# A recurrence whose input terms VectorE and ScalarE write into PSUM, in place of TensorE's injection products

## The chip, the core and the metric

The kernel runs on one core of a Trainium2 chip (trn2). The metric is the device time of one execution in microseconds. Five engines are spoken of: PE (TensorE), DVE (VectorE), ACT (ScalarE), POOL (GpSimd) and SP (SyncE, which only issues DMAs here).

## The reference

```python
def cell(h, x):
    gi = x @ W_ih + b_ih
    gh = h @ W_hh + b_hh
    i_r, i_z, i_n = jnp.split(gi, 3, axis=-1)
    h_r, h_z, h_n = jnp.split(gh, 3, axis=-1)
    r = jax.nn.sigmoid(i_r + h_r)
    z = jax.nn.sigmoid(i_z + h_z)
    n = jnp.tanh(i_n + r * h_n)
    h_new = (1.0 - z) * n + z * h
    return (h_new, h_new)
_, hs = jax.lax.scan(cell, initial_state, xs)
...
logits = flat_x @ Wg + bg
...
h = jax.nn.gelu(tok @ W1[i], approximate=False)
y = h @ W2[i] * p
out = out.at[sel_idx].add(y)
...
x = x + _L0_ffn_ref(_L0_cond_ref(cond_2048, x, ...), ...)
```

The input has 4 sequences of 512 positions and 512 features. A GRU runs over the 512 positions; its states (2048 rows) go to a router that gives each of four experts (512 to 2048 to 512 features) its 512 best rows; the experts' outputs are added to x. All in fp32 accuracy.

## The kernel before

**Segments.** The recurrence is cut into 16 segments per sequence (SEG = 16), so that 4 x 16 = 64 columns (COLS) advance together, 32 positions each (L = 32). As a segment's start isn't known, 8 steps of burn-in and one whole round of 32 go ahead of the round of 32 whose states count: FIRST + L = 72 steps, numbered 0 to 71. A check at the end would start further rounds; they aren't entered with this input.

**What is in a step.** The 512 features of the state are four blocks of 128 (j, or k where they are read). For each block j TensorE makes three gates (r, z, n) of 64 columns in PSUM bank j, `gate_ps`, as sums over the four blocks k of the old state. Numbers are scaled by powers of two and split into a high and a low half of 16 bits. In a rough step (i below ROUGH = 20) only high times high is made: 4 x 4 units of 3 products, 48. In an exact step a unit with the high half of the state takes both halves of the weights (6 products), one with the low half takes the high weights (3): 16 x 6 + 16 x 3 = 144 products of 128x128 by 64 columns, in the order of the table `ORDER`, chosen by hand. The unit (h, j, k) adds to gate bank j what state block k contributes; the last one of each j counts up `gates_mm`.

**Input terms.** x @ W_ih is made for all steps by 512-column products: chunk 3 of four ahead of the recurrence (L424 and L434, in fp32), the others by split halves, `fill` (L451), 24 products ahead of step 0 and then 18 in each step until step 22, which has 12. In a rough step they are dealt out over the k blocks (FILLS = 13, 2, 2, 1), in steps 20 to 22 they stand ahead of the step. ScalarE takes a finished tile of 512 columns out of banks 4 to 7 (`keep_tile`). Tiles of r and z land in a ring `gi_full`, and VectorE splits them in `rz_high` (L1128) and `rz_low` (L1135) into 16-bit halves `gi_rz`. Tiles of n stay fp32 in `gi`.

**Injection.** `inject` (L465 to L473) opens gate bank j of a step: TensorE multiplies `diag`, a diagonal matrix with the scale, by the step's 128 columns of `gi_rz`. It is one product in a rough step, two (high, low) in an exact one, and there a third (L472) adds the recurrent bias b_hn, which was loaded as a row and split by `split_bhn`. In a rough step VectorE adds b_hn instead, in L1248. An injection waits for `rn_done`: VectorE has read the bank's old gates.

**The other engines in a step** (block by block):

- ScalarE: `sig` (L779), one sigmoid of r and z, 128 columns; `tanh` (L784), 64 columns. Order: sig 0, sig 1, sig 2, tanh 0, tanh 1, sig 3, tanh 2, tanh 3. In 16 of the steps 29 to 48 it then squares a 512-wide piece of the first expert weights (L799), with an accumulator.
- VectorE: `reset` (L1245, r times the n gate), `candidate_in` (L1253), `one_less_z` (L1257, (z - 1) n), `blend` (L1264, the new state's high half), and in exact steps `keep_state` (L1269, the new state in fp32) and `low_part` (L1288, its low half for blocks 2 and 3). 16 instructions in a rough step, 22 in an exact one, in the order of the tuples `rough` and `exact`. `blend` and `keep_state` multiply by -s, a pointer scalar (`neg_scale`), and add.
- GpSimd: `carry` (L952, z times the old state) for four blocks, then `low_part` (L960) for blocks 0 and 1.

Each engine works its own list off in order; semaphores are all that ties them. From step 40 on TensorE makes the router's logits of the last state behind the gates (L479).

## Time and profile before

| | |
|---|---|
| median of 3 runs | 836.57 us (836.47 to 837.41) |
| profiled execution | 836.27 us, of which the span is 834.5 us |
| PE, DVE, ACT, POOL busy | 803.0, 619.8, 421.1, 179.9 us |
| granted TensorE clock, mean | 0.987 of full speed |
| first sigmoid of step 0 | at 61.2 us |
| last sigmoid of step 71 | at 439.3 us |

Times in the profile's rows are microseconds from the span's start, and then the duration; "x126" is the number of instructions merged into the row, and "[1.14 <-...]" the idle time of the engine before it and what ended it. PE rows are matmuls, PEld their weight loads. L numbers are lines of the kernel before.

### The profile page before, as it was taken

How to read it: one execution, taken by the hardware profiler on the slowest of the kernel's cores; microseconds unless marked ns; L12 is line 12 of the kernel's file. 1: busy time of each engine (PE TensorE's matmuls, PEld its weight loads, DVE VectorE, ACT ScalarE, POOL GpSimd, SP SyncE). 2: the span in 40 equal slices, each digit the busy share in tenths (PEclk: the TensorE clock that was granted, in tenths of full speed). 3: DMA queues.
4: the chain of work that ended last, by engine and by line, in shares of the span. 5: the costliest groups of instructions: out<-in, count | busy, mean ns of one | idle time of the engine just before them, and what ended most of it. 6: DMA issues, size and time to landing. Idle time of an engine off the chain costs nothing.

```text
span 834.5 us, 28320 instructions
## 1 busy us (share of the span) xinstructions
PE 803.0 (96%) x11781; PEld 528.0 (63%) x11782; DVE 619.8 (74%) x2113; ACT 421.1 (50%) x885; POOL 179.9 (22%) x459
## 2 busy tenths in 40 slices
PE   7999999999999999999995799999999999999996
PEld 3446556679999999999994444454445444444442
DVE  6979899878888888888888879767666676755300
ACT  0677666645566556554455448252835184417400
POOL 1002222123433334333330010121012101210011
PEclk9999999999999999999997899999999999999998
DMA  9810000000111010000001943471347224630022
GB/s 336 323 48 2 2 2 3 2 3 4 54 60 50 17 42 5 4 4 5 5 4 33 269 156 119 135 226 27 113 139 194 57 101 151 171 81 1 1 26 26
DMA packets 24286, 62.64 MB, mean 75 GB/s; under 512 B 4386, under 2 KB 4386, under 8 KB 22308
## 3 DMA queue, kind: packets, MB, share of 16 engines
q1 hardware_dynamic: 19312, 51.42, 18.1%
q0 software_dynamic: 3584, 8.42, 5.5%
q8 instruction: 87, 1.43, 0.7%
q10 hardware_dynamic: 1268, 1.08, 0.4%
q14 instruction: 35, 0.29, 0.1%
HBM read 52.50 MB, written 12.62 MB: 78 GB/s over the span
## 4 chain that ended last, share of the span: by engine, by line
PE 92%; DVE 5%; issue 1%; DMA 1%; ACT 0%; POOLq 0%; DVEq 0%
PE ps L459 29%; PE ps L666 20%; PE ps L680 20%; PE ps L451 10%; PE ps L469 3%; PE ps L434 3%; PE ps L424 2%; PE ps L600 1%; PE ps L653 1%; DVE big L1541 1%; PE ps L472 1%; DMA wa<-in_x_t 1%; DVE halves L1264 1%; DVE wa L1253 1%; PE ps L644 0%
## 5 line engine op out<-in xcount | busy, mean ns | idle before, releaser
L459 PE MATMUL ps<-halves,wa 128*128 128x64 f16 x8448 | 289.1, 193 | 1.4 <-DVE halves L1264 1.2
L459 PEld LDWEIGHTS ps<-halves,wa 128*128 128x128 f16 x8448 | 271.2, 98 | 20.2 <-DVE halves L1264 4.2
L680 PE MATMUL ps<-big 128*128 128x512 f16 x768 | 166.9, 379 | 0.0
L666 PE MATMUL ps<-hx,big 128*128 128x512 f16 x768 | 166.9, 379 | 0.0
L779 ACT ACTIVATE wa<-ps,un_gates 128x128 f32<-128x128 f32 x288 | 100.1, 365 | 111.0 <-PE ps L459 100.6
L680 PEld LDWEIGHTS ps<-big 128*128 128x128 f16 x768 | 75.1, 98 | 89.9
L666 PEld LDWEIGHTS ps<-hx,big 128*128 128x128 f16 x768 | 74.8, 98 | 90.0 <-issue 0.2
L784 ACT ACTIVATE wa<-wa,un_gates 128x64 f32<-128x64 f32 x288 | 97.4, 344 | 53.0 <-DVE wa L1253 48.9
L451 PE MATMUL ps<-hx,wb 128*128 128x512 f16 x432 | 106.9, 379 | 1.2 <-issue 1.1
L861 ACT ACTIVATE hx<-ps,un_hid_in 128x512 f32<-128x512 f32 x64 | 43.6, 682 | 109.2 <-PE ps L666 106.9
L1264 DVE SCALAR_TENSOR_TENSOR halves<-ocand,neg_scale,wa 128x64 f16<-128x64 f32 (+1 forms) x288 | 80.6, 280 | 4.4 <-issue 0.5
L1495 DVE SCALAR_TENSOR_TENSOR big<-wa,scale,big 128x2048 f16<-128x2048 f32 x28 | 65.3, 2350 | 21.1 <-ACT big L847 21.1
L1245 DVE TENSOR_TENSOR wa<-ps,wa 128x64 f32<-128x64 f32 x208 | 45.9, 221 | 43.4 <-ACT wa L779 43.4
L1253 DVE TENSOR_TENSOR wa<-wa,big 128x64 f32<-128x64 f32 x288 | 71.6, 249 | 5.1
L1629 DVE SCALAR_TENSOR_TENSOR big<-hx,hid_scale,big 128x512 f16<-128x512 f32 x64 | 47.8, 750 | 35.2 <-ACT big L864 29.0
L847 ACT ACTIVATE big<-wa,scale 128x2048 f16<-128x2048 f32 x28 | 54.8, 1988 | 34.1 <-DVEq L1483 34.1
L1441 DVE TENSOR_REDUCE chunk_peak<-wa 128x1 f32<-128x2048 f32 x28 | 62.3, 2279 | 4.5 <-DMA wa<-in_w 4.5
L469 PE MATMUL ps<-big,diag 128*128 128x128 f16 x496 | 63.5, 219 | 0.8 <-DVE wa L1245 0.4
L1257 DVE SCALAR_TENSOR_TENSOR ocand<-wa 128x64 f32<-128x64 f32 x288 | 63.5, 220 | 0.0
L451 PEld LDWEIGHTS ps<-hx,wb 128*128 128x128 f16 x432 | 37.9, 98 | 35.8 <-issue 1.9
L1018 POOL DMA_INDIRECT out<-hx,idx_out x16 | 29.0, 1815 | 136.1 <-DVE hx L1635 136.1
L952 POOL TENSOR_TENSOR wa<-wa,hx 128x64 f32<-128x64 f32 x128 | 40.9, 320 | 79.9 <-ACT wa L779 75.2
(221 smaller groups left out, 791.4 us busy)
## 6 DMA issues: line engine op xcount, KB each, us to landing
wa<-in_w SPq DMA_DIRECT2D x28, 1024.0 KB, 5.2
hs_rows<-big SPq DMA_DIRECT2D x8, 512.0 KB, 6.3
big<-in_w_hh SPq DMA_DIRECT2D x4, 768.0 KB, 19.6
wb<-in_w SPq DMA_DIRECT2D x12, 256.0 KB, 2.6
big<-in_w_ih SPq DMA_DIRECT2D x2, 1024.0 KB, 12.5
hx<-in_x_t SPq DMA_DIRECT2D x2, 1024.0 KB, 16.5
big<-in_w_ih ACTq DMA_DIRECT2D x2, 512.0 KB, 6.6
wa<-in_x_t SPq DMA_DIRECT2D x2, 512.0 KB, 6.2
```

What stands on the lines that cost most here:

```text
L451: mm = pe.matmul(ps[:, gi_bank(tile), :], wih_parts[:, w, k, m * P:(m + 1) * P], x_parts[:, q, t, k, :], start=(left == 0), stop=(left == ...
L459: mm = pe.matmul(gate_ps[:, j, g, :], whh_parts[:, k, w, (4 * g + j) * P:(4 * g + j + 1) * P], halves[:, src, k, h, :], start=False, stop= ...
L469: pe.matmul(gate_ps[:, j, 0:2, :], diag[:, :], gi_rz[:, c, j, part, :, cols], start=(part == HIGH), stop=False, skip_group_check=True)
L666: mm = pe.matmul(ps[:, m % 2, :], w1p[:, w, k, m * P:(m + 1) * P], tokT[:, t, k, :], start=(k == 0 and n == 0), stop=(k == KD - 1 and n == 2))
L680: mm = pe.matmul(ps[:, 2 + g % 2, :], hid[:, h, k, g * P:(g + 1) * P], w2p[:, w, k, :], start=(k == 0 and n == 0), stop=(k == KH - 1 and n ...
L779: act.activation(rz[:, j, :, :], gate_ps[:, j, 0:2, :], ACT.Sigmoid, scale=un_gates[:, 0:1]).then_inc(S["sig_done"], 1)
L784: act.activation(cand[:, j, :], cand_in[:, j, :], ACT.Tanh, scale=un_gates[:, 0:1]).then_inc(S["tanh_done"], 1)
L1253: dve.tensor_tensor(cand_in[:, j, :], rn[:, j, :], gi_n(j), ALU.add).then_inc(S["candin_ready"], 1)
L1257: dve.scalar_tensor_tensor(ocand[:, j, :], rz[:, j, 1, :], -1.0, cand[:, j, :], ALU.add, ALU.mult).then_inc(S["ocand_done"], 1)
L1264: dve.scalar_tensor_tensor(high_of(j), old(ocand_, j), neg_scale[:, 0:1], old(zh_, j), ALU.mult, ALU.add).then_inc(S["high_ready"], 1)
L1441: dve.tensor_reduce(chunk_peak[:, c:c + 1], stage[:, c * CHUNK:(c + 1) * CHUNK], AX.X, ALU.max, apply_absolute_value=True).then_inc(S["chu ...
L1495: dve.scalar_tensor_tensor(w_parts[which][:, LOW, cols], stage[:, cols], scale[:, which:which + 1], w_parts[which][:, HIGH, cols], ALU.mul ...
```

## The change

- TensorE's `inject` is gone, with `diag` and the split of b_hn (its two DMAs, a memset and eight small VectorE instructions).
- `gi_rz` holds fp32, laid out step by step (128 columns of r and z together). ScalarE writes finished tiles straight into it; `rz_high` and `rz_low` and ScalarE's first five copies are gone.
- A step's bank is now seeded: 128 columns of `gi_rz` times `seed_s` and 64 columns of b_hn are written into PSUM, and TensorE's products add to them. For steps 0 to 19 VectorE does it behind its blends, two instructions for each of four blocks (`seed`). For steps 20 on ScalarE does it behind its last tanh: `seed_most` for banks of blocks 0 to 2 (two instructions over three banks), `seed_last` for block 3 (two instructions).
- From step 23 (SWITCH) on odd steps use banks 4 to 6 for blocks 0 to 2 and even ones 0 to 2, so that `seed_most` works two steps ahead; bank 3 serves every step, and `seed_last` works one step ahead. The logits move from bank 4 to 7 and 0.
- In rough steps TensorE does all 18 fills first and then the gates block by block of j, not of k.
- GpSimd makes `wz` = s (1 - z) for each block (`taken`), behind each `carry`. VectorE's `one_less_z` becomes wz times n, `blend` and `keep_state` plain additions, and `reset` a plain product in rough steps too. In the exact order `keep_state` 0 and `one_less_z` 1 change places.

```diff
@@ tensor
-            def inject(j, c, cols, parts, steps):
-
-                pe.wait_ge(S["rn_done"], steps + j + 1)
-                for part in parts:
-                    pe.matmul(gate_ps[:, j, 0:2, :], diag[:, :], gi_rz[:, c, j, part, :, cols],
-                              start=(part == HIGH), stop=False, skip_group_check=True)
-                if LOW in parts:
-                    pe.matmul(gate_ps[:, j, 2, :], bhn_parts[:, j * P:(j + 1) * P], bhn_unit[:, :], start=False,
-                              stop=False, skip_group_check=True)
...
+                fill(filled(i), filled(i + 1))
+                for j in range(KD):
+                    pe.wait_ge(S["seeded_early"], 2 * (KD * i + j + 1))
+                    for k in range(KD):
+                        pe.wait_ge(S["high_ready"], made(i) + k + 1)
+                        unit(0, HIGH, j, k, src, (HIGH,), k == KD - 1)
...
+                    if j not in begun:
+                        begun.add(j)
+                        if j == KD - 1:
+                            pe.wait_ge(S["last_seeded"], half_steps + (2 - 2 * ROUGH))
+                        elif j == ORDER[0][1]:
+                            pe.wait_ge(S["seeded"], half_steps + (2 - 2 * ROUGH))
@@ scalar
+            def seed_most(bank, rows_of, before):
+
+                act.wait_ge(S["rn_done"], before)
+                act.activation(gate_banks[bank][:, :, 0:2 * COLS], rows_of(slice(0, KD - 1)), ACT.Copy,
+                               scale=seed_s[:, 0:1]).then_inc(S["seeded"], 1)
+                act.activation(gate_banks[bank][:, :, 2 * COLS:GATES],
+                               bhn_s[:, 0:KD - 1].unsqueeze(2).to_broadcast([P, KD - 1, COLS]), ACT.Copy
+                               ).then_inc(S["seeded"], 1)
+
+            def seed_last(rows_of, before):
+
+                act.wait_ge(S["rn_done"], before)
+                act.activation(last_gates[:, 0:2 * COLS], rows_of(KD - 1), ACT.Copy, scale=seed_s[:, 0:1]
+                               ).then_inc(S["last_seeded"], 1)
+                act.activation(last_gates[:, 2 * COLS:GATES], bhn_s[:, KD - 1:KD].to_broadcast([P, COLS]), ACT.Copy
+                               ).then_inc(S["last_seeded"], 1)
...
+            def seed_ahead(i):
+
+                if SWITCH <= i + 2 < FIRST + L:
+                    seed_most(bank_of(i + 2), rows_at(i + 2), KD * (i + 2))
+                if i + 1 < FIRST + L:
+                    seed_last(rows_at(i + 1), KD * (i + 2))
@@ gpsimd
+                def taken(j):
+
+                    pool.tensor_scalar(wz[:, j, :], rz[:, j, 1, :], neg_scale[:, 0:1], scale[:, STATE:STATE + 1],
+                                       ALU.mult, ALU.add).then_inc(S["wz_done"], 1)
+
...
+                exact = ((carry, 0), (taken, 0), (carry, 1), (taken, 1), (carry, 2), (taken, 2), (low_part, 0),
+                         (carry, 3), (taken, 3), (low_part, 1))
@@ vector
+            def seed(i, j):
+
+                c = (i // STEPS_C + CHUNK_ORDER[0]) % NC_
+                dve.tensor_scalar(gates_of(0, j)[:, 0:2 * COLS], gi_rz[:, c, j, i % STEPS_C, :], seed_s[:, 0:1], None,
+                                  ALU.mult).then_inc(S["seeded_early"], 1)
+                dve.tensor_copy(gates_of(0, j)[:, 2 * COLS:GATES], bhn_s[:, j:j + 1].to_broadcast([P, COLS])
+                                ).then_inc(S["seeded_early"], 1)
...
-                    dve.scalar_tensor_tensor(ocand[:, j, :], rz[:, j, 1, :], -1.0, cand[:, j, :],
-                                             ALU.add, ALU.mult).then_inc(S["ocand_done"], 1)
+                    dve.wait_ge(S["wz_done"], base + j + 1)
+                    dve.tensor_tensor(ocand[:, j, :], wz[:, j, :], cand[:, j, :], ALU.mult).then_inc(S["ocand_done"], 1)
...
-                    dve.scalar_tensor_tensor(high_of(j), old(ocand_, j), neg_scale[:, 0:1], old(zh_, j),
-                                             ALU.mult, ALU.add).then_inc(S["high_ready"], 1)
+                    dve.tensor_tensor(high_of(j), old(ocand_, j), old(zh_, j), ALU.add).then_inc(S["high_ready"], 1)
...
-                    dve.scalar_tensor_tensor(after(j), old(ocand_, j), neg_scale[:, 0:1], old(zh_, j),
-                                             ALU.mult, ALU.add).then_inc(S["state_done"], 1)
+                    dve.tensor_tensor(after(j), old(ocand_, j), old(zh_, j), ALU.add).then_inc(S["state_done"], 1)
```

ScalarE's list in a square step of the exact part, before: three sigmoids, two tanh, a sigmoid, two tanh, the square (L799), and the next step.

```order
L779 ACTIVATE wa<-ps,un_gates 128x128 x3
L784 ACTIVATE wa<-wa,un_gates 128x64 x2
L779 ACTIVATE wa<-ps,un_gates 128x128
L784 ACTIVATE wa<-wa,un_gates 128x64 x2
L799 ACTIVATE wa,sq<-wb 128x512
L779 ACTIVATE wa<-ps,un_gates 128x128 x3
```

And with the change (line numbers of the changed kernel: 775 is the sigmoid, 780 the tanh, 803 the square):

```order
L775 ACTIVATE wa<-ps,un_gates 128x128 x3
L780 ACTIVATE wa<-wa,un_gates 128x64 x2
L775 ACTIVATE wa<-ps,un_gates 128x128
L780 ACTIVATE wa<-wa,un_gates 128x64 x2
L746 ACTIVATE ps<-big,seed_s 128x3x128
L748 ACTIVATE ps<-bhn_s 128x3x64
L755 ACTIVATE ps<-big,seed_s 128x128
L757 ACTIVATE ps<-bhn_s 128x64
L803 ACTIVATE wa,sq<-wb 128x512
L775 ACTIVATE wa<-ps,un_gates 128x128 x3
```

Four writes into `ps` (PSUM) stand between the last tanh and the square.

TensorE's list over an exact step with logits, before (L479 logits, L469 and L472 injection, L459 recurrent products):

```order
L479 MATMUL ps<-wg_parts,halves 128x8 x4
L469 MATMUL ps<-big,diag 128x128 x2
L472 MATMUL ps<-bhn_unit,bhn_parts 128x64
L469 MATMUL ps<-big,diag 128x128 x2
L472 MATMUL ps<-bhn_unit,bhn_parts 128x64
L459 MATMUL ps<-halves,wa 128x64 x6
L469 MATMUL ps<-big,diag 128x128 x2
L472 MATMUL ps<-bhn_unit,bhn_parts 128x64
L459 MATMUL ps<-halves,wa 128x64 x12
L469 MATMUL ps<-big,diag 128x128 x2
L472 MATMUL ps<-bhn_unit,bhn_parts 128x64
L459 MATMUL ps<-halves,wa 128x64 x126
```

And with the change:

```order
L467 MATMUL ps<-wg_parts,halves 128x8 x4
L457 MATMUL ps<-halves,wa 128x64 x144
L467 MATMUL ps<-wg_parts,halves 128x8 x4
L457 MATMUL ps<-halves,wa 128x64 x144
```

The 144 products stand in their old order with nothing between them; the block of 126 begins with the unit (HIGH, 0, 1), the first that reads state block 1.

## Rows read from the trace of the kernel before

**Rows 1.** The page: the busy time of TensorE, and ScalarE's gelu over 512 columns

```profile
PE 803.0 (96%) x11781; PEld 528.0 (63%) x11782; DVE 619.8 (74%) x2113; ACT 421.1 (50%) x885; POOL 179.9 (22%) x459
...
L861 ACT ACTIVATE hx<-ps,un_hid_in 128x512 f32<-128x512 f32 x64 | 43.6, 682 | 109.2 <-PE ps L666 106.9
```

**Rows 2.** Chain of waits, from step 9's fills to step 10's: start, us, what

```profile
105.67 2.81 PE ps L451 x13
108.48 0.06 PE ps L469
...
109.48 0.35 PE ps L459 x12
...
111.18 0.86 PE ps L451 x4
```

**Rows 3.** Timeline, all engines, one exact step with logits: start us, us, instruction

```profile
402.19 1.16 ACT L779 ACTIVATE wa<-ps,un_gates 128x128 f32<-128x128 f32 x3 [1.61 <-PE ps L459]
402.59 0.22 DVE L1245 TENSOR_TENSOR wa<-ps,wa 128x64 f32<-128x64 f32 x1 [0.76 <-ACT wa L779]
...
403.93 0.27 PE L469 MATMUL ps<-big,diag 128*128 128x128 f16 x2
...
404.03 0.37 ACT L779 ACTIVATE wa<-ps,un_gates 128x128 f32<-128x128 f32 x1
...
404.07 0.28 PE L469 MATMUL ps<-big,diag 128*128 128x128 f16 x2
...
404.47 0.22 DVE L1245 TENSOR_TENSOR wa<-ps,wa 128x64 f32<-128x64 f32 x1
...
404.66 0.28 DVE L1264 SCALAR_TENSOR_TENSOR halves<-ocand,neg_scale,wa 128x64 f16<-128x64 f32 x1
404.75 0.36 POOL L960 TENSOR_TENSOR halves<-hx,halves 128x64 f16<-128x64 f32 x1
404.86 0.33 DVE L1253 TENSOR_TENSOR wa<-wa,big 128x64 f32<-128x64 f32 x1
...
405.10 3.88 PE L459 MATMUL ps<-halves,wa 128*128 128x64 f16 x126
...
405.23 0.35 ACT L784 ACTIVATE wa<-wa,un_gates 128x64 f32<-128x64 f32 x1 [0.60 <-DVE wa L1253]
...
406.42 0.41 DVE L1288 TENSOR_TENSOR halves<-hx,halves 128x64 f16<-128x64 f32 x2
407.18 1.16 ACT L779 ACTIVATE wa<-ps,un_gates 128x128 f32<-128x128 f32 x3 [1.60 <-PE ps L459]
...
409.02 0.37 ACT L779 ACTIVATE wa<-ps,un_gates 128x128 f32<-128x128 f32 x1
```

**Rows 4.** Timeline, VectorE, the last blend of rough step 8

```profile
109.13 0.28 DVE L1264 SCALAR_TENSOR_TENSOR halves<-ocand,neg_scale,wa 128x64 f16<-128x64 f32 x1
```

**Rows 5.** Groups of 20 to 60 us: count, busy us, mean ns, idle before

```profile
L1135 DVE TENSOR_TENSOR big<-gi_full,big 128x512 f16<-128x512 f32 x8 | 5.5, 690 | 0.5 <-DVE diag L1179 0.3
...
L753 ACT ACTIVATE big<-gi_full 128x512 f16<-128x512 f32 x5 | 3.1, 630 | 0.2
...
L730 ACT ACTIVATE hx<-hx,scale 128x512 f16<-128x512 f32 x4 | 2.5, 706 | 0.0
...
L1179 DVE TENSOR_SCALAR diag<-ident,un_gi 128x128 bf16<-128x128 f32 x1 | 0.3, 286 | 0.0
```

**Rows 6.** Groups of 300 to 400 us (20 exact steps)

```profile
L1264 DVE SCALAR_TENSOR_TENSOR halves<-ocand,neg_scale,wa 128x64 f16<-128x64 f32 x80 | 22.3, 279 | 0.0
...
L1257 DVE SCALAR_TENSOR_TENSOR ocand<-wa 128x64 f32<-128x64 f32 x80 | 17.5, 219 | 0.0
```

**Rows 7.** Timeline, ScalarE, behind the last tanh of a square step

```profile
229.62 0.61 ACT L799 ACTIVATE wa<-wb 128x512 f32<-128x512 f32 x1
230.14 0.19 ACT L799 ACTIVATION_READ_ACCUMULATOR wa<-wb 128x1 f32 x1
```

**Rows 8.** Timeline, TensorE, the first fills

```profile
50.57 8.15 PE L451 MATMUL ps<-hx,wb 128*128 128x512 f16 x37 [1.14 <-issue]
```

More of the change, by code:

```diff
@@ L27 @@
 ROUGH = 20
+SWITCH = 23
 FILLED = 24
@@ L961, in low_part @@
                                        ).then_inc(S["low_ready"], 1 + (KD - POOL_LOWS if j == POOL_LOWS - 1 else 0))
[L962 to L966 removed]
+                exact = ((carry, 0), (taken, 0), (carry, 1), (taken, 1), (carry, 2), (taken, 2), (low_part, 0),
+                         (carry, 3), (taken, 3), (low_part, 1))
+                rough = ((carry, 0), (taken, 0), (carry, 1), (taken, 1), (carry, 2), (taken, 2), (carry, 3),
+                         (taken, 3))
+                for f, j in exact if low else rough:
+                    f(j)
             def held(i):
@@ L1206, in whh_low @@
+            for j in range(KD):
+                seed(0, j)
             def whh_low(n):
@@ L1228, in w1_peak, with step @@
                 dve.tensor_reduce(peak[:, W1:W1 + 1], sq[:, :], AX.X, ALU.max).then_inc(S["w_peak"], 1)
-            def step(gi_n, after, src, base, low, moved=False, ahead=(), between=(), bias_added=True):
+            def step(gi_n, after, src, base, low, bank, moved=False, between=(), following=None):
                 dst = 1 - src
@@ L1351, in _ @@
                     between.append((w1_peak, 0))
-                step(lambda j, c=c, cols=cols: gi[:, c, j, 2, cols], after, i % 2, KD * i, i >= ROUGH - 1, moved, ahead, between,
-                     i >= ROUGH)
+                step(lambda j, c=c, cols=cols: gi[:, c, j, 2, cols], after, i % 2, KD * i, i >= ROUGH - 1, bank_of(i), moved,
+                     between, i + 1 if i + 1 < ROUGH else None)
             def run(steps):
```

251 lines of the change are left out of this document (97 added, 154 removed).

## The prediction

> **What bounds the kernel now.** I read the page first: TensorE is busy for 96% of the span [rows 1], so the question at every place is whether TensorE really has work there or is only just being fed. The recurrence has 72 steps: 20 rough ones (0 to 19), then 52 exact ones (20 to 71), of which 20 to 22 still carry fill products. I went through them kind by kind, since each has another limit.
>
> In a **rough step** the chain of waits stays on TensorE throughout [rows 2]: 13 fills take 2.81 us (0.216 each), an injection 0.06, twelve recurrent products 0.35 (0.029 each). From one block of 13 fills to the next it is 111.18 - 105.67 = 5.51 us. The rest of it is 5 more fills and 48 products in all: 18 x 0.216 + 48 x 0.029 + 4 x 0.055 = 5.50. Such a step is TensorE's work and nothing else.
>
> An **exact step** lasts 4.99 us, first sigmoid to first sigmoid, 402.19 to 407.18 [rows 3]. TensorE's own work in it: 126 products in 3.88 us, of which the last one's 0.19 is depth, so 0.0293 each and 144 x 0.0293 = 4.22; four injections of three products, 404.07 - 403.93 = 0.14 each, 0.56; and some 0.1 for the logits. That is 4.9 of 4.99. But VectorE closes nearly the same circle: its first product starts 0.40 after the sigmoid (402.59), its last low half ends at 406.42 + 0.41 = 406.83, 4.24 later, and the next first sigmoid comes 0.35 after that. 0.40 + 4.24 + 0.35 = 4.99. So the reader should see two circles closed at once; taking the injections away cannot give all of its 0.56.
>
> **The change, part by part.**
>
> *Rough steps.* Four injections leave TensorE, 4 x 0.055 = 0.22 us, so 5.51 becomes 5.29. All 18 fills now stand ahead of the gates. What has to fit under them is the elementwise work: in the old order the last blend ended at 109.13 + 0.28 = 109.41 [rows 4]. In the new order the gate products take 48 x 0.029 = 1.4, the last sigmoid comes some 2.2 after their start (after the second tanh), and the blend about 2.1 later: 4.3. Then VectorE writes eight seeds. The four products I price by a 128-wide scaling, 0.286 [rows 5], and the four bias copies by a 64-wide operation, 0.219 [rows 6]; with the overlap of 0.09 between neighbours that ScalarE shows [rows 7], 4 x (0.20 + 0.13) = 1.3 at the least, 2.0 if nothing overlaps. The first pair is there by 4.7 and the fills end at 1.4 + 3.9 = 5.3, so 0.6 us cover it. If that cover were gone, each 0.1 beyond it costs 2 us in 20 steps. What VectorE loses is a 512-wide cast and subtraction in about every step (0.69 for the subtraction alone) [rows 5], so its load stays about the same. Gain: 20 x 0.22 = **4.4 us**.
>
> *Start.* TensorE stands still for 1.14 us before its first fill [rows 8], while VectorE ends the last low part of x. Ahead of that part stand three subtractions of 0.69 us [rows 5] on VectorE, which the change drops; x is then ready before TensorE is. Gain **1.1 us**. The removed DMAs, memset and splitting of b_hn stand on ACT's queue and on VectorE beside work of TensorE: nothing.
>
> *Steps 20 to 22.* Fills (18, 18 and 12 of them, 3.9 to 2.6 us) stand ahead of the gates and cover ScalarE's seeds for the next step. The injections' 0.56 is all gain: **1.7 us**.
>
> *Steps 23 to 71*, 48 periods. TensorE alone would need 4.3. VectorE: the eight sums lose their pointer scalar. A sum with it takes 279 ns, an operation of the same size with a constant 219 [rows 6], a plain product 0.22 (404.47); I take 0.06 off each, 0.48 in all, and VectorE's circle closes in 4.51. A third circle then ends last. The fourth sigmoid (404.03) is followed after 0.44 by the fourth product on VectorE (404.47), and the second blend is queued behind that (404.66). TensorE's block of 126 products begins with the first one that needs this second blend, and its end (405.10 + 3.88 = 408.98) starts the next fourth sigmoid at 409.02 [rows 3]. Today the injections hide this circle: the blend is done at 404.94, the block starts at 405.10. Without them: 0.40 + 0.19 + 0.22 for sigmoid, product and blend, 0.06 for TensorE to notice, 3.88 for the block, 0.04 to the sigmoid: **4.79**, 0.20 less than now.
>
> *ScalarE in these steps* gets four writes into PSUM behind the fourth tanh. The trace has no ScalarE instruction that writes PSUM; I price them by width. 128 columns with a scale pointer take 0.37, 512 columns 0.682, so 0.82 ns a column [rows 1, 3]; a scale pointer costs 706 - 630 = 76 ns [rows 5]; neighbours overlap by 0.09, since the square of 0.61 is followed after 0.52 [rows 7]. 384 columns: 0.58; 192 without pointer: 0.37; 128: 0.37; 64 without: 0.26. The sum less four overlaps is 1.2 us. Its ends are 1.0 (four times the narrowest) and 1.7 (the two three-bank writes at the price of 512 columns). The fourth tanh starts at 405.23; less 0.1 for the faster step, plus 0.26, ScalarE is free at 405.39 and the next sigmoid is due at 407.18 - 0.20 = 406.98. There is room for 1.6, so 1.2 costs nothing, and 1.7 costs 0.1. The Trainium skill (ScalarE: Activation LUTs, Step-by-step: what each stage is for) says that PSUM is ScalarE's lower-latency destination; by that the sum would be at its lower end, and no run here shows it.
>
> *The 16 square steps.* In 16 of the 48 a 512-wide square and its accumulator read, 0.52 + 0.19 = 0.71 [rows 7], follow the seeds. Then ScalarE's own circle is the longest: sigmoid to VectorE 0.40, first to fourth product 404.47 - 402.59 = 1.88 less 0.12 for two cheaper sums, fourth product to fourth tanh 0.76 less 0.06, tanh 0.26, seeds 1.2, square 0.71: 5.04 against 4.99 now. So these steps give nothing and lose 16 x 0.05 = **0.8**; the other 32 give 32 x 0.20 = **6.4**.
>
> *GpSimd* makes s(1-z) for each block: 4 more instructions beside 4 and 2, each priced like its neighbour at 404.75, 0.36, less overlap [rows 3]. At most 3.6 us in 4.8, in an order that has each ready before its tanh is. The router's split in step 10 and everything behind the recurrence stay as they are.
>
> Sum: 4.4 + 1.1 + 1.7 + 6.4 - 0.8 = 12.8. The profiled execution took 836.27 us (its span 834.5 and 1.8 around it), 0.3 under the median of 836.57. 836.3 - 12.8 = **823.5 us**.
>
> **The rivals.**
>
> *GpSimd holds VectorE up.* The fourth addition (404.86) took 0.33 where its like take 0.22; it began 0.1 after a GpSimd instruction (404.75) [rows 3]. There are now ten such instructions in a step for six. If one more falls on the third circle, a period grows by 0.11: 48 x 0.11 = 5.3, giving 828.8; two give 834. Against it: the operations of the third circle are few, and VectorE's own circle has 0.28 to spare. The Trainium skill (SBUF — State Buffer, Who interferes with whom) has a rule for it: a VectorE instruction with two SBUF inputs and a GpSimd one that reads SBUF exclude each other for its whole length. By that, each new instruction would cost somebody up to 0.3; the trace shows 0.11, and only where VectorE comes just behind. Chance 0.18.
>
> *ScalarE becomes the bound (slower).* With s for the seeds, its circle is 3.12 + s without and 3.83 + s with a square. The other gains, 7.2 us, are used up where 32 (s - 1.87) + 16 (s - 1.16) = 7.2, at s = 1.78. At 2.0 us the kernel takes 836.3 - 7.2 + 4.2 + 13.4 = 846.7. For it: writes that cross three banks are in no row, and 1.78 is just past my upper end. Chance 0.07.
>
> *VectorE bounds the rough steps.* If eight seeds and half of a weight split outlast the cover by 0.3, 20 steps give 6 back: 829.5. Against it is the 0.6 of cover above. Chance 0.12.
>
> *The seeds are not what limits anything and the third circle is shorter*, because the low halves of step i no longer hold TensorE: 4.72 rather than 4.79, squares at 4.9: 4 us less, 819. Chance 0.05.
>
> **How the numbers follow.** My forecast has 0.58. A measurement of this kernel tells a difference from 0.2% (1.7 us) on. The range 815 to 833 takes in the forecast with s at 1.7 (832.8: squares 0.55 and the others 0.04 slower than now or than forecast), one delay by GpSimd, the VectorE rival and the faster case; outside are the ScalarE rival and combinations of two. Slower than now by over 0.2% takes s above 1.8 or two delays on top of a rough-step loss: 0.07. Within 0.2%: 0.03. Faster: 0.90.
>
> **What would show it.** In the changed profile: rough steps 5.29 apart, with no gap on TensorE ahead of the gates; no idle time ahead of the first fill; steps with logits 4.79 apart, TensorE idle ahead of the product that needs the second blend; square steps near 5.0, with the sigmoid coming straight behind the accumulator read; the 3x128 write near 0.58 us. It is wrong if sigmoids in ordinary exact steps start without idle time on ScalarE, if TensorE waits for a rough step's seeds, or if blends still take 0.28.

## The result, and the profile after

The changed kernel takes **841.5 us** (median of 5 runs, 841.31 to 842.4) against 836.9 for the kernel before beside it: ratio 1.0057, 95% interval [1.0042, 1.0071]. It is slower. 823.5 was forecast, with a range of 815 to 833.

The page of the changed kernel, for [rows 1]: the span, busy times, the chain by engine and two groups (line, engine, operation, busy us, mean ns, idle before it and what ended that).

```profile
span 839.5 us, 27870 instructions
...
PE 792.9 (94%) x11077; PEld 501.5 (60%) x11078; DVE 616.1 (73%) x2205; ACT 481.8 (57%) x1088; POOL 301.7 (36%) x747
...
PE 62%; DVE 25%; ACT 7%; issue 4%; DMA 1%; POOL 0%; POOLq 0%; DVEq 0%; ACTq 0%
...
L457 PE MATMUL ps<-halves,wa 128*128 128x64 f16 x8448 | 282.1, 193 | 16.8 <-DVE halves L1260 13.6
```

TensorE has 10 us less to do, as meant, and stands still longer: its recurrent products now wait 16.8 us, most of it for VectorE's blends. GpSimd's load went from 180 to 302 us. VectorE holds 25% of the chain that ended last.

By the first sigmoids of the steps the span divides like this (us):

| stretch | before | after | difference | predicted |
|---|---|---|---|---|
| start to step 20 | 174.07 | 173.71 | -0.4 | -5.5 |
| steps 20 to 22 | 20.99 | 20.22 | -0.8 | -1.7 |
| steps 23 to 71, 48 periods | 242.36 | 247.44 | +5.1 | -5.6 |
| step 71 to the end | 397.1 | 398.2 | +1.1 | 0 |

The first row hides two opposite parts: step 0's first sigmoid comes 2.5 earlier (58.72 for 61.19), and the 20 rough steps behind it take 115.0 for 112.9, 2.1 more.

**A rough step after.** The chain of waits through rough step 13 to 14, for [rows 2] (start, us, what):

```profile
133.85 0.15 DVE wa L1236
...
137.00 0.23 DVE halves L1260
137.23 0.27 DVE ps L1189
137.50 0.13 DVE ps L1191
...
138.38 0.25 DVE ps L1189
138.63 0.13 DVE ps L1191
138.76 0.65 DVE wa L1203
139.41 0.15 DVE wa L1236
```

TensorE is gone from it. The circle is VectorE's own: from reset product to reset product 139.41 - 133.85 = 5.56 us, of which the step's arithmetic takes 3.38 (to 137.23), the eight seeds 1.53, a split of a recurrent weight 0.65. The next step's first product, whose sigmoid ended at 138.6, stands behind the seeds and the split until 139.4. The timeline shows what becomes of GpSimd there:

```profile
144.22 0.74 DVE L1203 SCALAR_TENSOR_TENSOR wa<-big,scale,wa 128x512 f16<-128x512 f32 x1
144.25 0.88 POOL L968 TENSOR_TENSOR wa<-wa,halves 128x64 f32<-128x64 f32 x1 [2.12 <-ACT wa L775]
```

A product that elsewhere takes GpSimd 0.32 takes 0.88, because it began 0.03 behind VectorE's 0.74.

**An exact step after.** The timeline from the first sigmoid (400.15) to the next step's first (405.29), with the fourth at 401.99, for [rows 3]:

```profile
400.15 1.15 ACT L775 ACTIVATE wa<-ps,un_gates 128x128 f32<-128x128 f32 x3 [0.57 <-PE ps L457]
...
400.60 0.32 POOL L968 TENSOR_TENSOR wa<-wa,hx 128x64 f32<-128x64 f32 x1 [1.68 <-ACT wa L775]
...
401.64 0.48 POOL L972 TENSOR_SCALAR wa<-wa,neg_scale,scale 128x64 f32<-128x64 f32 x1
...
401.99 0.37 ACT L775 ACTIVATE wa<-ps,un_gates 128x128 f32<-128x128 f32 x1
...
402.22 0.26 DVE L1254 TENSOR_TENSOR ocand<-wa 128x64 f32<-128x64 f32 x1
...
402.56 0.21 DVE L1236 TENSOR_TENSOR wa<-ps,wa 128x64 f32<-128x64 f32 x1
...
403.05 0.32 POOL L968 TENSOR_TENSOR wa<-wa,hx 128x64 f32<-128x64 f32 x1
...
403.20 0.35 ACT L780 ACTIVATE wa<-wa,un_gates 128x64 f32<-128x64 f32 x1 [0.61 <-DVE wa L1249]
403.36 0.43 POOL L972 TENSOR_SCALAR wa<-wa,neg_scale,scale 128x64 f32<-128x64 f32 x1
...
403.46 0.57 ACT L746 ACTIVATE ps<-big,seed_s 128x384 f32<-128x384 f32 x1
...
403.89 0.25 DVE L1254 TENSOR_TENSOR ocand<-wa 128x64 f32<-128x64 f32 x1
...
404.52 0.41 DVE L1282 TENSOR_TENSOR halves<-hx,halves 128x64 f16<-128x64 f32 x2
405.29 0.37 ACT L775 ACTIVATE wa<-ps,un_gates 128x128 f32<-128x128 f32 x1 [0.58 <-PE ps L457]
```

GpSimd works without a gap from 400.60 to 404.05. Its second s(1-z) ends at 402.12, so the candidate product of block 1 starts at 402.22, and the reset product of block 3, queued behind it, at 402.56: 0.57 behind its sigmoid, 0.44 in [rows 3]. Its fourth s(1-z) ends at 403.79, 0.24 after its tanh (403.55), and the last candidate product waits for it until 403.89. The step takes 5.13 us for 4.99.

These rows close a circle of GpSimd's own. From the first sigmoid to its first instruction 0.45, nine instructions without a gap to the end of the fourth s(1-z) 3.19, 0.10 to the last candidate product, 1.04 to the end of VectorE's last low part (404.93), 0.36 to the next first sigmoid: 5.14, the whole step.

The groups of 300 to 400 us price the parts, for [rows 6]:

```profile
L972 POOL TENSOR_SCALAR wa<-wa,neg_scale,scale 128x64 f32<-128x64 f32 x77 | 33.5, 435 | 0.0
...
L968 POOL TENSOR_TENSOR wa<-wa,hx 128x64 f32<-128x64 f32 x77 | 25.6, 332 | 32.3 <-ACT wa L775 32.3
L1254 DVE TENSOR_TENSOR ocand<-wa 128x64 f32<-128x64 f32 x78 | 21.3, 272 | 1.4 <-ACT wa L780 0.2
L1260 DVE TENSOR_TENSOR halves<-ocand,wa 128x64 f16<-128x64 f32 x78 | 19.9, 255 | 0.4 <-issue 0.3
...
L1264 DVE TENSOR_TENSOR hx<-ocand,wa 128x64 f32<-128x64 f32 x79 | 17.6, 222 | 0.0
...
L746 ACT ACTIVATE ps<-big,seed_s 128x384 f32<-128x384 f32 x20 | 11.3, 566 | 0.0
...
L755 ACT ACTIVATE ps<-big,seed_s 128x128 f32<-128x128 f32 x20 | 7.0, 350 | 0.0
L748 ACT ACTIVATE ps<-bhn_s 128x192 f32<-128x192 f32 x20 | 6.2, 310 | 0.0
...
L757 ACT ACTIVATE ps<-bhn_s 128x64 f32<-128x64 f32 x20 | 4.1, 203 | 0.0
```

The plain sums are cheap (222 for the kept state); the candidate product grew from 219 to 272.

### The profile page after: what moved, and what is told of

Its sections match the earlier page's. It is cut to its first block, busy times and chain, and to the rows that moved or that the text cites. A ratio compares the mean times of both kernels' runs of the same rounds, so it can differ in the third digit from the quotient of the medians.

```text
span 839.5 us, 27870 instructions
## 1 busy us (share of the span) xinstructions
PE 792.9 (94%) x11077; PEld 501.5 (60%) x11078; DVE 616.1 (73%) x2205; ACT 481.8 (57%) x1088; POOL 301.7 (36%) x747
## 4 chain that ended last, share of the span: by engine, by line
PE 62%; DVE 25%; ACT 7%; issue 4%; DMA 1%; POOL 0%; POOLq 0%; DVEq 0%; ACTq 0%
PE ps L644 20%; PE ps L658 20%; PE ps L457 13%; DVE wa L1236 5%; DVE wa L1249 5%; DVE ocand L1254 4%; DVE halves L1260 3%; PE ps L432 3%; PE ps L449 2%; DVE ps L1189 2%; ACT wa L775 2%; PE ps L422 2%; ACT wa L803 1%; DVE ps L1191 1%; DVE wa L1203 1%
## 5 line engine op out<-in xcount | busy, mean ns | idle before, releaser
L457 PE MATMUL ps<-halves,wa 128*128 128x64 f16 x8448 | 282.1, 193 | 16.8 <-DVE halves L1260 13.6
L457 PEld LDWEIGHTS ps<-halves,wa 128*128 128x128 f16 x8448 | 260.5, 98 | 45.1 <-DVE halves L1260 19.2
L775 ACT ACTIVATE wa<-ps,un_gates 128x128 f32<-128x128 f32 x288 | 104.2, 366 | 48.1 <-PE ps L457 37.4
L972 POOL TENSOR_SCALAR wa<-wa,neg_scale,scale 128x64 f32<-128x64 f32 x288 | 125.3, 435 | 0.0
L1236 DVE TENSOR_TENSOR wa<-ps,wa 128x64 f32<-128x64 f32 x288 | 62.7, 218 | 51.8 <-ACT wa L775 51.8
L449 PE MATMUL ps<-hx,wb 128*128 128x512 f16 x432 | 97.0, 379 | 0.1
L1249 DVE TENSOR_TENSOR wa<-wa,big 128x64 f32<-128x64 f32 x288 | 76.5, 266 | 5.0
L1254 DVE TENSOR_TENSOR ocand<-wa 128x64 f32<-128x64 f32 x288 | 74.8, 260 | 3.9 <-issue 0.4
L1260 DVE TENSOR_TENSOR halves<-ocand,wa 128x64 f16<-128x64 f32 (+1 forms) x288 | 71.7, 249 | 4.4 <-issue 0.3
L1033 POOL DMA_INDIRECT hx<-hs_rows,idx x16 | 16.3, 1016 | 130.6 <-DVE idx L1598 96.3
```

Of the source, the lines that this page charges most:

```text
L449: mm = pe.matmul(ps[:, gi_bank(tile), :], wih_parts[:, w, k, m * P:(m + 1) * P], x_parts[:, q, t, k, :], start=(left == 0), stop=(left == ...
L457: mm = pe.matmul(gates_of(bank, j)[:, g * COLS:(g + 1) * COLS], whh_parts[:, k, w, (4 * g + j) * P:(4 * g + j + 1) * P], halves[:, src, k, ...
L775: act.activation(rz[:, j, :, :], gates_of(bank, j)[:, 0:2 * COLS].rearrange("p (g c) -> p g c", g=2), ACT.Sigmoid, scale=un_gates[:, 0:1]) ...
L972: pool.tensor_scalar(wz[:, j, :], rz[:, j, 1, :], neg_scale[:, 0:1], scale[:, STATE:STATE + 1], ALU.mult, ALU.add).then_inc(S["wz_done"], 1)
L1236: dve.tensor_tensor(rn[:, j, :], gates_of(bank, j)[:, 2 * COLS:GATES], rz[:, j, 0, :], ALU.mult).then_inc(S["rn_done"], 1)
L1249: dve.tensor_tensor(cand_in[:, j, :], rn[:, j, :], gi_n(j), ALU.add).then_inc(S["candin_ready"], 1)
```

## The experiments

Every kernel was compared with the kernel before on the same chip. The theory after the result: GpSimd's s(1-z) costs the exact steps (A), and the seeds on VectorE cost the rough ones. Its rivals: ScalarE's writes into PSUM, or the two bank sets, hold the steps.

**1. The change without GpSimd's part.**

```diff
-dve.tensor_tensor(ocand[:, j, :], wz[:, j, :], cand[:, j, :], ALU.mult)
+dve.scalar_tensor_tensor(ocand[:, j, :], rz[:, j, 1, :], -1.0, cand[:, j, :], ALU.add, ALU.mult)
 (both sums with neg_scale again; GpSimd without taken(j))
```

> The changed kernel without GpSimd's s(1-z): one_less_z, blend and keep_state as before, all seeds as in the change. Theory A (GpSimd's ten instructions close a circle of 5.13 us in an exact step; the fourth s(1-z) is what VectorE waits for): ordinary exact steps fall to the 4.79 of the third circle, square steps lie near 5.0, and the time falls by 8 to 12 us against the changed kernel, to 829 to 833. Theory B (the seeds on ScalarE, or writing PSUM while TensorE works, hold the exact steps at 5.13): the steps stay above 5.0 and the time stays within 3 us of 841. Rough steps: VectorE-bound in both, 5.4 to 5.7.

Measured: 833.3 us, ratio 0.9948 [0.9931, 0.9966]. Exact steps 4.93 us, rough ones 5.56 as in the changed kernel. Taking this part out gives 8 us back, so it is what made the change slower. The writes into PSUM and the two bank sets are still there, so they don't hold the step at 5.13 (theory B). 4.93 and not 4.79, though: my expectation forgot that the sums become dear again, so something of VectorE's holds the step.

**2. GpSimd's part alone, on the kernel before** (injections, order and diagonal stay).

> The kernel before with GpSimd's s(1-z) and plain sums alone; injections stay. Theory A: exact steps rise from 4.99 to at least 5.13, as GpSimd's circle has no TensorE injection in it, +7 us or more over 52 steps; rough steps stay at 5.51 since TensorE bounds them: 843 to 847 in all. Theory B: plain sums shorten VectorE's circle and the time is 837 or a little less.

Measured: 843.9 us, ratio 1.0082 [1.0065, 1.0098]; exact steps 5.14, rough ones 5.51. The same price in both surroundings: 0.15 a step here, 0.20 between run 1 and the changed kernel.

**3. ScalarE writes the rough steps' seeds too** (all but step 0's).

```diff
-if ROUGH <= i + 1 < SWITCH:
+if 1 <= i + 1 < SWITCH:
     (ScalarE: seed_most and seed_last for step i + 1)
-between, i + 1 if i + 1 < ROUGH else None)
+between, None)
```

> The changed kernel with ScalarE writing the seeds of steps 1 to 19 too, as it does for 20 to 22; GpSimd's part stays. If VectorE's eight writes are what makes rough steps 5.56 (the chain of waits shows only VectorE there), they fall to TensorE's 5.29: 19 x 0.27 and the late steps 2, 7, 8 and 11 shorter, 6 to 8 us, 834 to 836 in all. If instead ScalarE's order or the wait for s(1-z) holds them, they stay over 5.45 and the time changes by less than 3 us.

Measured: 839.6 us, ratio 1.0035 [1.0023, 1.0046]. Most rough steps without a split of x now alternate between 5.0 and 5.5, 5.26 on average, and step 20 comes 2.9 us earlier (170.8 for 173.7). Exact steps stay at 5.13. The cause is as expected, the size is a miss: 1.9 us in the time, not 6 to 8, as the eight steps in which ScalarE also splits x now take 5.6 to 6.3.

**4. Runs 1 and 3 together.**

> Both edits: no s(1-z) on GpSimd, ScalarE writes all seeds but step 0's. Theory A: the two gains are separate and add: rough steps 5.29, exact 4.79, square steps 5.0, 822 to 826 in all. Theory B: no better than e3.

Measured: **827.0 us**, ratio 0.9873 [0.9856, 0.9889], faster than both kernels, with nothing left out. Exact steps 4.93, step 20 at 169.7. That is 1 us above the range of theory A, and yet more than the two gains added up (8.2 and 1.9): without s(1-z) the alternating rough steps take 4.84 and 5.32, where run 3 has 5.02 and 5.50. The eight rough steps that split x take 5.5 to 5.9; the chain of waits names ScalarE there:

```profile
68.51 0.47 ACT ps L751
68.98 0.25 ACT ps L753
69.23 0.29 ACT ps L760
69.53 0.14 ACT ps L762
69.67 1.18 ACT big L720 x2
70.85 0.61 ACT hx L710
71.46 0.26 ACT wa L780
```

Seeds (1.15 us), two evictions of the input product and the high half of an x tile stand in one row ahead of the next sigmoid. So ScalarE does become a bound, but only once VectorE is out of the way, and in the steps that split x.

**5. Constant scale in the sums.** Run 4 had left 4.93 open.

```diff
-dve.scalar_tensor_tensor(high_of(j), old(ocand_, j), neg_scale[:, 0:1], old(zh_, j), ...
+dve.scalar_tensor_tensor(high_of(j), old(ocand_, j), -128.0, old(zh_, j), ...
 (keep_state alike)
```

> The best kernel so far (ScalarE writes all seeds but the first step's; GpSimd makes no s(1-z)) with the scale of the two sums written as the constant -128.0 instead of read through a [P,1] pointer. This input's state scale is 128, so nothing is left out for it; for another input it would be. It tells what bounds an exact step at 4.93 us once GpSimd is out of the way. Theory A (VectorE's circle is the bound, and the pointer is what its sums cost over a plain sum): a sum takes 0.22 us for 0.28, eight of them give back 0.48, VectorE's circle goes to 4.45 and the third circle (fourth sigmoid, fourth product, second blend, 126 products) ends last at 4.79: 48 x 0.14 = 6.7 us under the best kernel's 827.0, so 820.3. Theory B (the third circle as I drew it is wrong, the seeds on ScalarE or TensorE's own 144 products hold the step at 4.93): sums are cheaper, steps stay 4.93, 826 to 827. Theory C (only the sum takes the pointer's price in part): steps at 4.86, 824.

Measured: 819.9 us, ratio 0.9805 [0.9788, 0.9821]. Ordinary steps 4.79: theory A to 0.4 us. ScalarE's writes and the two bank sets are in this kernel too, so they don't hold a step above 4.79. A sum takes 238 to 242 ns on average for 277 to 286.

```profile
L1270 DVE SCALAR_TENSOR_TENSOR hx<-ocand,wa 128x64 f32<-128x64 f32 x83 | 20.0, 242 | 0.0
L1265 DVE SCALAR_TENSOR_TENSOR halves<-ocand,wa 128x64 f16<-128x64 f32 x83 | 19.7, 238 | 0.3 <-issue 0.3
```

So the gain that the change sought by plain sums is real; what it paid for them cost more.

**6. Constants in GpSimd's s(1-z)**, nothing else changed.

```diff
-pool.tensor_scalar(wz[:, j, :], rz[:, j, 1, :], neg_scale[:, 0:1], scale[:, STATE:STATE + 1],
+pool.tensor_scalar(wz[:, j, :], rz[:, j, 1, :], -128.0, 128.0,
```

> The changed kernel with GpSimd's s(1-z) written with the constants -128.0 and 128.0 instead of two [P,1] pointers (right for this input alone). In the changed kernel the instruction takes 0.435 us, a product of two tensors beside it 0.33, and GpSimd is busy without a gap from the first to the fourth s(1-z), which VectorE's last candidate product waits for. Theory A (GpSimd's run of instructions sets the step; the pointers are what the price is over 0.33): four instructions get 0.07 to 0.10 cheaper, the fourth s(1-z) is ready 0.3 to 0.4 earlier, until the fourth tanh (0.24 earlier than it) ends last: the step goes from 5.13 to 4.89 or less, 48 x 0.24 = 11.5 us less, so 830. Theory B (GpSimd's price is its start-up and does not depend on pointers): 0.435 stays, steps stay 5.13, 841.5. Between them, the time moves by 48 x 4 x what an instruction gets cheaper.

Measured: 827.1 us, ratio 0.9889 [0.9873, 0.9906]. The instruction falls from 435 to 243 ns, most exact steps to 4.87. Theory A, further than I had it:

```profile
L972 POOL TENSOR_SCALAR wa<-wa 128x64 f32<-128x64 f32 x81 | 19.7, 243 | 0.0
```

The instruction behind it starts 0.22 later (399.99 to 400.21) where it was 0.37 (400.90 to 401.27), so the saving is in the queue too, not only in the recorded span. Two pointers to one number each turned a gain of 9 us into a loss of 5.

**7 and 8. s(1-z) for blocks 0 and 1 only**, and the same with ScalarE's three-bank writes ahead of the fourth tanh.

```diff
+if j >= 2:  (the old forms of ocand and of both sums)
-exact = ((carry, 0), (taken, 0), (carry, 1), (taken, 1), (carry, 2), (taken, 2), (low_part, 0), (carry, 3), (taken, 3), ...
+exact = ((carry, 0), (taken, 0), (carry, 1), (taken, 1), (carry, 2), (carry, 3), (low_part, 0), (low_part, 1))
```

> The best kernel so far, with GpSimd's s(1-z) and plain sums for blocks 0 and 1 alone; blocks 2 and 3 use the old forms. GpSimd's order is zh0, s(1-z)0, zh1, s(1-z)1, zh2, zh3, low0, low1. Nothing is left out. Theory A (GpSimd's ten instructions in a row were what cost the changed kernel its exact steps, and VectorE's dear sums what bounds the best kernel so far): GpSimd's run ends 0.87 earlier, nothing waits for it; VectorE's circle is 4 x 0.06 shorter, 4.69 for 4.93; the third circle ends last at 4.79 to 4.83: 48 x 0.12 = 5.8 under 827.0, so 821.2 (819 to 823). Theory B (VectorE and GpSimd shut each other out, so that two more GpSimd instructions cost VectorE what the cheaper sums give back): 4.93, 827. Theory C (low0 and low1, behind zh3 in this order, come too late for TensorE): 5.0, 830.

> The same with ScalarE's three-bank writes for the step after next put between its third and fourth tanh instead of behind the fourth (the fourth tanh then starts some 0.0 to 0.3 later in every exact step, and ScalarE's tail behind it is 0.8 shorter). It tells whether ScalarE's tail bounds the square steps once the others have got faster. Theory A (in the 16 square steps ScalarE's circle of 5.04 less what VectorE gives, about 4.9, would be the bound, the idle time between third and fourth tanh, which is some 0.3, takes in only part of the writes of 0.75): ordinary steps get 0.2 to 0.4 slower and square steps no faster: 48 x 0.3 = 14 us more than the kernel without, 835. Theory B (TensorE's products of the third circle hide it): within 1.5 us of the kernel without.

Measured: 833.7 (0.9973 [0.9962, 0.9984]) and 834.9 us (0.9985 [0.9976, 0.9995]); exact steps 5.06 in both. A miss: worse than run 4 by 6.7, and than all three theories of run 7. The place of ScalarE's writes does not matter (theory B of run 8). In run 7's timeline the second s(1-z) starts at 405.66 and takes 0.48, the candidate product of block 1 waits for it until 406.24, and the reset product starts 0.55 behind its sigmoid. Half of GpSimd's new work holds the place that matters just as the whole did.

**9. s(1-z) ahead of z x h**, the changed kernel otherwise.

```diff
-exact = ((carry, 0), (taken, 0), (carry, 1), (taken, 1), (carry, 2), (taken, 2), (low_part, 0), (carry, 3), (taken, 3), ...
+exact = ((taken, 0), (carry, 0), (taken, 1), (carry, 1), (taken, 2), (carry, 2), (low_part, 0), (taken, 3), (carry, 3), ...
```

> The changed kernel with nothing altered but GpSimd's order: s(1-z) ahead of z x h for each block. Nothing is left out. In all ten kernels so far an exact step is the time from the last sigmoid's start to the end of VectorE's last low part, and 0.357 + 1.837 = 2.194 us behind it; the first part is 2.797 before, 2.939 in the changed kernel, 2.677 with constants on GpSimd. Theory A (GpSimd's four s(1-z), not its load as such, hold VectorE: the second is 0.12 late for the product ahead of reset 3, the fourth 0.35 late for the last product, while z x h is needed one VectorE instruction later): each s(1-z) is ready 0.32 earlier, reset 3 starts 0.45 after the sigmoid for 0.57, the last product at its tanh's end; first part 2.68 to 2.72, steps 4.87 to 4.91, 48 x 0.24 = 11.5 us less: 830. Theory B (VectorE and GpSimd shut each other out; who comes first in the queue does not matter): steps 5.10 or more, 840 to 842.

Measured: 832.6 us, ratio 0.9951 [0.9935, 0.9968]; most exact steps 4.92. Order alone gives back 9 us and turns the change from slower into faster. The timeline around the fourth sigmoid (400.58):

```profile
400.58 0.37 ACT L775 ACTIVATE wa<-ps,un_gates 128x128 f32<-128x128 f32 x1
...
400.74 0.21 DVE L1254 TENSOR_TENSOR ocand<-wa 128x64 f32<-128x64 f32 x1
...
401.05 0.21 DVE L1236 TENSOR_TENSOR wa<-ps,wa 128x64 f32<-128x64 f32 x1
```

The candidate product of block 1 starts 0.16 behind the sigmoid for 0.23, the reset product 0.47 for 0.57.

**10. One pointer:** s(1-z) as (z - 1) x (-s).

```diff
-... neg_scale[:, 0:1], scale[:, STATE:STATE + 1], ALU.mult, ALU.add)
+... -1.0, neg_scale[:, 0:1], ALU.add, ALU.mult)
```

> The changed kernel with s(1-z) as (z - 1) x (-s), one [P,1] pointer and one constant on GpSimd instead of two pointers; the value is the same, as s is a power of two. Two pointers take 0.435 us, two constants 0.243. Theory A (each pointer costs the same): 0.34 an instruction, half of what the constants gave in time, 841.5 - 7 = 834.3. Theory B (one pointer or two is the same, as the operand is read in one go): 0.43, steps 5.13, 841. Theory C (the first is free): 0.25, 827.

Measured: 838.2 us, ratio 1.0021 [1.0011, 1.0030]. The price is as theory A had it, half way:

```profile
L972 POOL TENSOR_SCALAR wa<-wa,neg_scale 128x64 f32<-128x64 f32 x79 | 26.6, 337 | 0.0
```

The time is not (838.2 for 834.3): steps stay at 5.12. The fourth s(1-z) is ready only 0.10 earlier and the last candidate product still waits for it: GpSimd now stands still for 0.29 ahead of the low part of block 0, which reads VectorE's kept state, and the last z x h and s(1-z) are queued behind that. And five of VectorE's instructions are drawn out in place of four (table below).

**11. Runs 9, 10 and 3 together.**

> Both of those together, and all seeds of the rough steps but the first written by ScalarE: the changed kernel's whole idea with GpSimd's form and order mended, valid for every input. Theory A: exact steps 4.80 to 4.87 (plain sums make the part from the last sigmoid 0.06 to 0.12 shorter than the best general kernel's 2.738), rough steps as in the kernel whose seeds ScalarE writes: 839.6 - 48 x 0.28 = 826, so level with the best general kernel's 827.0 or up to 4 us under it (823 to 827). Theory B (GpSimd's ten instructions cost VectorE in collisions what the plain sums give): exact steps 4.93 or more, 829 or more.

Measured: 834.9 us, ratio 0.9984 [0.9975, 0.9994]; exact steps 5.10. Theory B, and worse: mended order and mended price do not add up. Two instructions ahead of the reset product of block 3 are now drawn out to 0.37 (of 0.22), and it starts 0.63 behind its sigmoid.

**12. Low part of block 2 on GpSimd**, on run 4.

```diff
-LOW_BY = "PPDD"
+LOW_BY = "PPPD"
```

> The best general kernel so far (827.0) with the low part of block 2 made by GpSimd instead of VectorE. Nothing is left out. In every kernel so far an exact step is the time from the last sigmoid to the end of VectorE's last low part and 2.194 us behind it; here VectorE has one instruction of 0.20 less in that part, 2.738 becomes 2.54. Theory A (that part is the bound until TensorE's block of 126 products takes over, 0.857 to the end of the second blend and 3.944 behind it as in the kernel with constant sums): 4.80, 48 x 0.13 = 6.3 us less, 820.7. With one more VectorE instruction stalled 0.13 by GpSimd's new one: 4.87, 824. Theory B (an exact step at 4.93 is TensorE's or ScalarE's own): 4.93, 827. Theory C (block 2's low part from GpSimd comes later than VectorE's last one): 5.0 or more, 830.

Measured: 832.6 us, ratio 0.9954 [0.9940, 0.9967]; exact steps 5.02. Theory C's time, in the main by another cause. The last kept state and the last low part in run 4, then here, with the last candidate product ahead of them:

```profile
402.77 0.27 DVE L1270 SCALAR_TENSOR_TENSOR hx<-ocand,neg_scale,wa 128x64 f32<-128x64 f32 x1
...
402.96 0.41 DVE L1289 TENSOR_TENSOR halves<-hx,halves 128x64 f16<-128x64 f32 x2
```

```profile
400.35 0.31 POOL L988 TENSOR_TENSOR halves<-hx,halves 128x64 f16<-128x64 f32 x1 [0.49 <-DVE hx L1270]
400.39 0.35 DVE L1258 SCALAR_TENSOR_TENSOR ocand<-wa 128x64 f32<-128x64 f32 x1
...
401.05 0.27 DVE L1270 SCALAR_TENSOR_TENSOR hx<-ocand,neg_scale,wa 128x64 f32<-128x64 f32 x1
401.07 0.41 POOL L988 TENSOR_TENSOR halves<-hx,halves 128x64 f16<-128x64 f32 x1 [0.42 <-DVE hx L1270]
...
401.43 0.23 DVE L1289 TENSOR_TENSOR halves<-hx,halves 128x64 f16<-128x64 f32 x1
```

From the kept state's start to the last low part's end it is 0.60 in run 4 and 0.61 here. The removed instruction had stood in a gap: the last low part waits for the kept state of its own block to be written. What the step loses comes earlier: the last candidate product takes 0.35, where it takes 0.21 in run 4. It is not GpSimd's new instruction (401.07) that stands beside it but the old low part of block 1, which here starts 0.04 ahead of it and in run 4 0.02 behind it (medians). TensorE does wait for the new low part too (0.13), but then again for VectorE's last one (0.07), so that wait does not set the step.

**What holds an exact step.** Over some 26 exact steps of each kernel (42 to 69; medians in us, instructions of VectorE drawn out by over 0.07, and GpSimd's busy us, as means of a step; exact steps of runs 2 and 3 are as the changed kernel's, those of 8 as 7's):

| kernel | last sigmoid to end of last low part | exact step | drawn out | GpSimd busy | time |
|---|---|---|---|---|---|
| before | 2.797 | 4.992 | 1.0 | 1.99 | 836.9 |
| changed | 2.939 | 5.133 | 4.0 | 3.68 | 841.5 |
| 1, without s(1-z) | 2.738 | 4.933 | 1.0 | 1.94 | 833.3 |
| 4, and ScalarE seeds | 2.738 | 4.933 | 1.0 | 1.93 | 827.0 |
| 5, constant sums | 2.591 | 4.790 | 2.9 | 1.97 | 819.9 |
| 6, constants on GpSimd | 2.677 | 4.870 | 4.9 | 2.96 | 827.1 |
| 7, half | 2.868 | 5.062 | 2.8 | 2.87 | 833.7 |
| 9, s(1-z) first | 2.731 | 4.926 | 3.1 | 3.67 | 832.6 |
| 10, one pointer | 2.923 | 5.117 | 5.0 | 3.28 | 838.2 |
| 11, 9 + 10 + 3 | 2.904 | 5.098 | 5.0 | 3.33 | 834.9 |
| 12, low part 2 moved | 2.825 | 5.017 | 2.0 | 2.31 | 832.6 |

In every row the step is the second column and 2.19 to 2.20 us. Those are 0.36 from the end of the last low part to the next first sigmoid and 1.84 from the first to the fourth sigmoid, and neither changed in any kernel, with injections or without. The sum alone proves nothing, since the three parts make up a step by definition; that two of them stay the same suggests that the step ends through VectorE's last low part. The starts of TensorE's products bear it out. They lie 0.029 apart where nothing holds them, and at the first product that reads the last low part there is a hole in every kernel but one: 0.03 beyond that before and in run 6, 0.07 in run 12, 0.09 to 0.10 in the others. In **run 5** there is none. There TensorE waits 0.17 ahead of the block of 126 products, for the second blend, and then runs through: the third circle as it was forecast. (Most others wait there too, but then once more for the last low part.)

What sets the second column differs:

- Before and in runs 1, 4 and 12 it is VectorE's own row of instructions behind the last sigmoid.
- In the changed kernel and in runs 2, 3, 9 and 10 the last candidate product starts 0.10 behind the end of the fourth s(1-z), and VectorE stands still for it. In all but run 10 GpSimd has worked without a gap since the first sigmoid, so its queue closes the circle: 0.445 + 3.186 + 0.103 + 1.042 + 0.357 = 5.133 in the changed kernel and 0.471 + 2.865 + 0.103 + 1.128 + 0.357 = 4.924 in run 9, which has one z x h less ahead of the fourth s(1-z).
- In runs 7 and 8 VectorE waits in the same way for the second s(1-z), and no longer behind it.
- In runs 6 and 11 it doesn't wait for the fourth one; five instructions drawn out are what is left of GpSimd's price there.

## Why the prediction was wrong

**Direction and size.** Wrong in both. 0.07 had been given to slower. Two of the rivals came true at once (GpSimd holds VectorE up, 0.18; VectorE bounds the rough steps, 0.12), and the first was more expensive than its price there, 0.11 a period. Of the three signs of being wrong one appeared: TensorE waits for a rough step's seeds. ScalarE has idle time ahead of the sigmoids of ordinary exact steps (0.57), and blends take 255 ns and not 279.

**Start: right.** TensorE no longer stands still ahead of the first fill; the fills of step 1 begin at 59.57 us for 61.25. These 1.68 are the 1.14 of [rows 8], step 0's 0.22 and 0.3 more. The 0.3 mean nothing: the first sigmoid lies between 58.2 and 59.9 in the kernels that share this start.

**Rough steps: the cover was mis-sized.** TensorE's share was right: the first two steps are 5.29 apart. But "the first pair is there by 4.7 and the fills end at 5.3, so 0.6 us cover it" failed. The arithmetic, from the gate products' start (137.68) to the last blend's end (142.79), takes 5.1, not 4.3. Some 0.7 of the 0.8 between come from the queue: I had counted seeds and split as load, and not asked who stands behind them. It is the next step's first reset product. Eight seeds take 1.53, where I had 1.3 to 2.0. With the seeds on ScalarE the 20 rough steps take 109.8 us for 115.0 (run 4 for run 1). GpSimd has a share in these steps too: with the seeds still on VectorE most of them take 5.46 and 5.40 where s(1-z) is made cheaper (runs 6 and 10) and 5.48 where it comes first (run 9), for 5.56.

**Steps 20 to 22: right for two.** 8.65 became 8.08 and 7.35 became 6.82, the 0.56 of the injections. The third went from 4.98 to 5.31. That is ScalarE's doing in the main: its last eviction of an input tile (0.76, at 191.92) stands ahead of its four writes, and the next sigmoid (193.93) comes straight behind them; without s(1-z), in run 1, it is 5.24. So the rival that ScalarE becomes the bound came true in one step.

**Exact steps: the step that failed** is the sentence on GpSimd, "each priced like its neighbour at 404.75, 0.36", and "in an order that has each ready before its tanh is". The instruction took 0.435, since it reads two pointers; the fourth was ready 0.24 after its tanh, at the end of nine instructions without a gap, and the last candidate product had to wait for it; and what the second delayed was not a blend but the reset product queued behind it. I had added up GpSimd's load (3.6 of 4.8) and not laid its ten instructions out against VectorE's, nor asked what stands between the fourth s(1-z) and the next sigmoid: 3.6 fit into 4.8, but the circle that they close is 5.13. Against run 1, which has neither s(1-z) nor the cheaper sums, this part costs 0.20 a step. The other 0.14 up to the forecast of 4.79 is VectorE's: run 1 without the cheaper sums takes 4.93, run 5 with them 4.79.

**VectorE's circle: cheaper, then spent.** Its undisturbed instructions fell from 5.19 to 4.75 us a step, 0.44 of the 0.48 forecast. What they are drawn out by rose from 0.27 to 0.59.

**The third circle: right, but seldom the bound.** It sets the step in run 5, at the forecast 4.79, with some luck in its terms: blend behind product 0.14 for 0.19, the blend itself 0.30 for 0.22. The product stands at 0.40, as the sum had it, but at 0.44 or 0.45 before and in runs 1 and 4, and at 0.44 in the very row that the sum read. In the other kernels the circle over VectorE's last low part is longer, and the forecast had VectorE done by 4.51. From the last sigmoid to the last low part run 5 got 0.15 of the 6 x 0.06 = 0.36 that the six sums behind the reset product promised: two more instructions were drawn out. More would not have helped, since TensorE's block holds that step at 4.79.

**ScalarE: right.** Its four writes run from 403.46 to 404.71, 1.25 us for 1.2. 384 columns into PSUM take 0.566 for 0.58, 128 columns 0.35 for 0.37; 192 and 64 without a pointer 0.31 and 0.20 for 0.37 and 0.26. By the rule of the Trainium skill (ScalarE: Activation LUTs, Step-by-step: what each stage is for) that PSUM is the lower-latency destination, the sum should have lain at its lower end, 1.0; only the narrow writes lean that way. The square steps did not show as a kind of their own: they are at 5.13 like the others, with ScalarE 0.02 short of being their bound (the sigmoid starts 0.11 behind the accumulator read, 0.09 where nothing stands between). In runs 5, 6 and 9 they do show, at 4.89, 4.94 and 5.02, the sigmoid straight behind the accumulator read; 5.04 had been forecast.

**Not forecast.** The period of step 23 became 1.3 us shorter (6.31 to 5.02), with the splits that stood in it; the other 47 take 6.4 more, 0.135 each. The stretch behind the recurrence took 1.1 longer; it varies by more among the kernels (397.3 to 398.8 in runs 1 to 12), and I did not follow it up.

**Left open:** what the drawing out would cost alone. In the changed kernel it is lateness that ends last: run 9 changes the order at an unchanged load, has the fourth s(1-z) ready 0.30 earlier behind the last sigmoid and gets 0.21 of a step back, 0.09 being lost behind it. In runs 6 and 11 nothing waits for it, and five instructions are drawn out instead of one. No run has the lateness without the drawing out. Nor is it worked out why run 11, with s(1-z) first and one pointer, ends at 5.10 and run 6, with constants in the old order, at 4.87.

## What to carry to other kernels

Work moved to an idle engine is not free because that engine has room: lay its instructions out in time against their consumer's queue, and ask for each which instruction stands behind the one that would wait. Look for the circle that the step closes (here: last sigmoid to last low part) and test it in more than one kernel before you price a saving; an instruction in a gap of it is worth nothing. Expect it to change with the kernel: the changed one closed through GpSimd's queue, run 5 through TensorE's block. And price the exact form: of GpSimd's 0.435 us two pointer operands made up 0.19.
